# Fourier block MLP on one core: the layer groups in twos, with the 64-row matmuls of two groups side by side

## The reference

```python
xf = jnp.fft.rfft2(x, axes=(1, 2), norm='ortho')          # -> (B, H, 65, 8, 96), complex
o1r = relu(xr @ w1[0] - xi @ w1[1] + b1[0])
o1i = relu(xi @ w1[0] + xr @ w1[1] + b1[1])
o2r = o1r @ w2[0] - o1i @ w2[1] + b2[0]
o2i = o1i @ w2[0] + o1r @ w2[1] + b2[1]
o = softshrink(stack([o2r, o2i]), 0.01)
out = jnp.fft.irfft2(complex(o), s=(H, W), norm='ortho') + x
```

## Time and profile before

| | |
|---|---|
| median of 3 runs | 5096.25 us (5095.34 to 5097.84) |
| span of the profiled execution | 5094.2 us; no time of its own is given beside the span |
| granted TensorE clock, mean | 0.993 |
| TensorE busy | 4981.3 us (98%) |
| VectorE busy | 3816.7 us (75%) |
| ScalarE busy | 2996.3 us (59%) |
| GpSimd busy | 1436.3 us (28%) |
| DMA moved | 430.24 MB, mean 84 GB/s |

### The profile page before, as it was taken

How to read it: one execution, slowest core, us unless ns; L and a number is a source line. 1 busy time by engine, 2 the same in 40 slices (tenths; PEclk the granted TensorE clock), 3 DMA queues, 4 the chain that set the end, 5 groups by cost and what they waited for, 6 DMA issues and landing times.

```text
span 5094.2 us, 113221 instructions
## 1 busy us (share of the span) xinstructions
PE 4981.3 (98%) x40000; PEld 4673.3 (92%) x40000; DVE 3816.7 (75%) x6159; ACT 2996.3 (59%) x5409; POOL 1436.3 (28%) x905
## 2 busy tenths in 40 slices
PE   6999999999999999999999999999999999999997
PEld 6999999999999999999999999999999999999996
DVE  5777777777777777777777777777777777777876
ACT  4555655556655566555566555665556655556653
POOL 3033223332123332233321333312333123332220
PEclk8999999999999999999999999999999999999998
DMA  5044423444323443234442344432344323444233
GB/s 114 12 94 105 98 59 69 91 105 105 68 57 87 105 105 87 56 81 94 105 105 52 70 90 105 106 70 62 79 105 106 86 61 78 92 105 105 61 73 72
DMA packets 1699712, 430.24 MB, mean 84 GB/s; under 512 B 1698848, under 2 KB 1698976, under 8 KB 1699104
## 3 DMA queue, kind: packets, MB, share of 16 engines
q1 hardware_dynamic: 1696768, 421.83, 37.5%
q10 hardware_dynamic: 2336, 0.59, 0.1%
HBM read 220.84 MB, written 201.33 MB: 83 GB/s over the span
## 4 chain that ended last, share of the span: by engine, by line
PE 96%; DVE 2%; issue 1%; SPq 1%; ACT 0%; DMA 0%; DVEq 0%; ACTq 0%
PE psum L807 15%; PE psum L778 14%; PE psum L822 14%; PE psum L760 13%; PE psum L849 13%; PE psum L832 9%; PE psum L790 7%; PE psum L859 3%; PE psum L860 3%; PE psum L861 3%; DVE mixed L655 1%; SPq L387 1%; DVE spectrum L628 0%; PE psum L840 0%; PE psum L839 0%
## 5 line engine op out<-in xcount | busy, mean ns | idle before, releaser
L655 DVE COPY mixed<-psum 128x768 f32<-128x768 f32 (+1 forms) x512 | 477.4, 932 | 700.0 <-PE psum L790 700.0
L541 ACT ACTIVATE sums_high<-psum 128x512 fp32r<-128x512 f32 x768 | 459.2, 599 | 731.3 <-PE psum L849 731.2
L807 PEld LDWEIGHTS psum<-mats,mixed 128*128 128x128 f32 x6272 | 744.0, 191 | 121.2 <-issue 113.1
L807 PE MATMUL psum<-mats,mixed 128*128 128x128 f32 x6272 | 841.8, 283 | 0.0
L778 PE MATMUL psum<-w_whole,whole 128*128 128x192 f32 x4160 | 782.3, 330 | 40.9 <-ACT whole L482 11.4
L822 PE MATMUL psum<-w2t,hidden 128*128 128x192 f32 x4160 | 771.7, 328 | 0.0
L849 PE MATMUL psum<-mats,spectrum 128*128 128x128 f32 x6144 | 743.7, 275 | 3.1 <-DVE spectrum L663 1.6
L760 PE MATMUL psum<-mats,x 128*128 128x128 f32 x6144 | 704.9, 277 | 33.6 <-DVE x L582 17.8
L760 PEld LDWEIGHTS psum<-mats,x 128*128 128x128 f32 x6144 | 696.0, 193 | 40.9 <-issue 23.0
L778 PEld LDWEIGHTS psum<-w_whole,whole 128*128 128x128 f32 x4160 | 673.3, 197 | 60.6 <-issue 33.7
L849 PEld LDWEIGHTS psum<-mats,spectrum 128*128 128x128 f32 x6144 | 714.5, 192 | 4.1 <-DVE sums_low L701 2.0
(11 more groups left out here) (76 smaller groups left out, 7800.7 us busy)
## 6 DMA issues: line engine op xcount, KB each, us to landing
x<-x SPq DMA_DIRECT2D x736, 192.0 KB, 2.9
out<-x SPq DMA_DIRECT2D x736, 192.0 KB, 2.5
x<-x SPq DMA_DIRECT2D x736, 64.0 KB, 2.6
out<-x SPq DMA_DIRECT2D x736, 64.0 KB, 2.2
x<-x SPq DMA_DIRECT2D x32, 144.0 KB, 2.7
out<-x SPq DMA_DIRECT2D x32, 144.0 KB, 2.3
w2t<-L_conv_w SPq DMA_DIRECT2D x124, 36.0 KB, 1.8
x<-x SPq DMA_DIRECT2D x64, 48.0 KB, 2.4
```

The lines of the kernel that those rows point to most:

```text
L655: copied = dve.tensor_copy(mixed[s % 2][:, 0:k], both_b(s)[:, 0:k])
L807: last = pe.matmul(out[tile], flat[:, tile * SIZE:(tile + 1) * SIZE], mat(FH), start=True, stop=True)
```

## The change

The groups are handled in rounds of two, ten rounds (`ROUNDS`) in a unit. Round j takes the even group 2j and the odd groups around it. What it does:

- TensorE has one stretch of 64-row matmuls in a round: `stage_b_halved(2j)`, `stage_d_middle(2j - 2)`, `stage_d_middle(2j - 1)`, `stage_b_halved(2j + 1)`. The steps over 128 rows follow in the order first layer of the odd group, `stage_c` even, outer tiles of the odd group before, first layer of the next even group, `stage_c` odd, outer tiles even.
- For odd groups the halved part now opens the sums in PSUM and the whole part closes them; likewise the outer tiles of odd groups now close the second layer's sums and increment `d_done`. `stage_b_halved` of an odd group above 1 waits for `b_copied` of the even group just before it.
- ScalarE and VectorE follow the new order. `gather` is split in `gather_whole` and `gather_halved`.
- Each `unfold_step` is cut in two (16 steps over 5 or 6 rows), and `spare(k)` places four steps in each round from round 1 on: the 16 unfold steps in rounds 1 to 4, the six prepare steps in rounds 5 and 6.

No matmul is added or taken away. The core of the diff (ScalarE's round first, then the unfold step, VectorE's round, TensorE's stages and TensorE's round):

```diff
+ROUNDS = NS // 2 + 2
+
+
+def even_group(j):
+    return 2 * j if 0 <= 2 * j < NS else None
+
+
+def odd_group(j):
+    return 2 * j + 1 if 0 <= 2 * j + 1 < NS else None
...
+                for j in range(ROUNDS):
+                    if j == 0:
+                        gather_halved(1)
+                        gather_whole(1)
+                    if even_group(j - 1) is not None:
+                        hide(even_group(j - 1))
+                    if odd_group(j - 2) is not None:
+                        exceed(odd_group(j - 2))
+                    if j > 0 and odd_group(j) is not None:
+                        act.wait_ge(b_done, n * NS + 2 * j)
+                        gather_whole(odd_group(j))
+                        gather_halved(odd_group(j))
+                    if odd_group(j - 1) is not None:
+                        hide(odd_group(j - 1))
+                    if j == ROUNDS - 1:
+                        act.wait_ge(flip_done, n + 1)
+                        act.activation(U[:, 0:BLOCK, SIZE + 2:].rearrange("p c k -> p k c"), bank_flip,
+                                       ACT.Copy).then_inc(flip_copied, 1)
+                    if even_group(j - 1) is not None:
+                        exceed(even_group(j - 1))
+                    if even_group(j + 1) is not None:
+                        act.wait_ge(b_done, n * NS + (2 * j + 1))
+                        gather_whole(even_group(j + 1))
+                        gather_halved(even_group(j + 1))
...
-                x_unit, (lo, hi) = xs[par], PIECES[k // 2]
+                p, what = divmod(k, 4)
+                x_unit, (lo, hi) = xs[par], PIECES[p]
+                lo, hi = ((lo, lo + 5), (lo + 6, hi))[what % 2]
...
+                    dve.wait_ge(unfold_even, n * (2 * NP) + (2 * p + what - 1))
...
+                    if what == 3:
+                        done.then_inc(unfolded, 1)
...
+                for j in range(ROUNDS):
+                    if odd_group(j - 1) is not None:
+                        mix(odd_group(j - 1))
+                    if even_group(j - 1) is not None:
+                        hide_middle(even_group(j - 1))
+                    if 0 < j:
+                        spare(4 * j - 4)
+                        spare(4 * j - 3)
+                    if odd_group(j - 2) is not None:
+                        shrink(odd_group(j - 2))
+                    if odd_group(j - 1) is not None:
+                        seed(odd_group(j - 1))
+                        hide_middle(odd_group(j - 1))
+                    if 0 < j:
+                        spare(4 * j - 2)
+                    if even_group(j) is not None:
+                        mix(even_group(j))
+                    if 0 < j:
+                        spare(4 * j - 1)
+                    if even_group(j - 1) is not None:
+                        shrink(even_group(j - 1))
+                    if even_group(j) is not None:
+                        seed(even_group(j))
...
+                opens = s % 2 == 0
...
-                    pe.matmul(bank_b(s, k), whole[s % 2][:, k // 2, :, k % 2], w1_whole[par][:, :, :].rearrange("p r o -> p (r o)"),
-                              start=k % 2 == 0, stop=False, skip_group_check=True)
+                    last = pe.matmul(bank_b(s, k), whole[s % 2][:, k // 2, :, k % 2], w1_whole[par][:, :, :].rearrange("p r o -> p (r o)"),
+                                     start=opens and k % 2 == 0, stop=not opens, skip_group_check=True)
+                if not opens:
+                    last.then_inc(b_done, 1)
...
+                opens = s % 2 == 1
...
+                    if opens and s > 1:
+                        pe.wait_ge(b_copied, n * NS + s)
...
-                                             start=False, stop=True, skip_group_check=True)
-                last.then_inc(b_done, 1)
+                                             start=opens and i == 0, stop=not opens, skip_group_check=True)
+                if not opens:
+                    last.then_inc(b_done, 1)
...
+                ends = s % 2 == 1
                 pe.wait_ge(relu_done, n * (2 * NS) + (2 * s + 1))
-                pe.wait_ge(seeded, n * NS + (s + 1))
+                if not ends:
+                    pe.wait_ge(seeded, n * NS + (s + 1))
...
+                ends = s % 2 == 0
                 pe.wait_ge(middle_done, n * NS + (s + 1))
+                if not ends:
+                    pe.wait_ge(seeded, n * NS + (s + 1))
...
-                for s in range(NS + 2):
-                    if s < NS:
-                        stage_b_whole(par, n, s)
-                    if s == NS:
+                for j in range(ROUNDS):
+                    if odd_group(j - 1) is not None:
+                        stage_b_whole(par, n, odd_group(j - 1))
+                    if j == ROUNDS - 1:
+                        stage_d_outer(par, n, odd_group(j - 2))
+                    if even_group(j - 1) is not None:
+                        stage_c(n, even_group(j - 1))
+                    if j < ROUNDS - 1 and odd_group(j - 2) is not None:
+                        stage_d_outer(par, n, odd_group(j - 2))
+                    if even_group(j) is not None:
+                        stage_b_whole(par, n, even_group(j))
+                    if odd_group(j - 1) is not None:
+                        stage_c(n, odd_group(j - 1))
+                    if j == ROUNDS - 1:
                         flip(n)
-                        stage_c(n, NS - 1)
-                    if s >= 2:
-                        stage_d_outer(par, n, s - 2)
-                        stage_d_middle(par, n, s - 2)
-                    if s < NS:
-                        stage_b_halved(par, n, s)
-                    if 1 <= s < NS:
-                        stage_c(n, s - 1)
+                    if even_group(j - 1) is not None:
+                        stage_d_outer(par, n, even_group(j - 1))
+
+                    if even_group(j) is not None:
+                        stage_b_halved(par, n, even_group(j))
+                    if even_group(j - 1) is not None:
+                        stage_d_middle(par, n, even_group(j - 1))
+                    if odd_group(j - 1) is not None:
+                        stage_d_middle(par, n, odd_group(j - 1))
+                    if odd_group(j) is not None:
+                        stage_b_halved(par, n, odd_group(j))
```

More of the change, by code:

```diff
@@ L469, in _, with gather_whole @@
         def _(act):
-            def gather(s):
-                w, h, first = whole[s % 2], halved[s % 2], GROUPS[s][0]
+            def gather_whole(s):
+                w, first = whole[s % 2], GROUPS[s][0]
+                j = 2 + 2 * first
                 if s == REAL:
@@ L509, in layers @@
                 act.wait_ge(dve_copied, (n + 1) * len(A_DVE))
[L510 removed]
+                gather_whole(0)
                 act.wait_ge(w_loaded[par], (m + 1) * W_LOADS * 16)
[L512 to L534 removed]
@@ L535, in layers, with hide @@
-                act.wait_ge(flip_done, n + 1)
-                act.activation(U[:, 0:BLOCK, SIZE + 2:].rearrange("p c k -> p k c"), bank_flip,
-                               ACT.Copy).then_inc(flip_copied, 1)
+                def hide(t):
+                    tiles = hidden[t % 2]
+                    act.wait_ge(c_done, n * NS + (t + 1))
+                    act.activation(tiles[:, 0, 0:pairs(t)], bank_c[:, 0, 0:pairs(t)], ACT.Relu,
+                                   bias=b1t[par][:, 0:1]).then_inc(relu_done, 1)
+                    k = pairs(t) if None not in GROUPS[t] else 1
+                    act.activation(tiles[:, 1, 0:k], bank_c[:, 1, 0:k], ACT.Relu,
+                                   bias=b1t[par][:, 2:3]).then_inc(relu_done, 1)
@@ new lines, in exceed @@
+                def exceed(t):
+                    act.wait_ge(d_done, n * NS + (t + 1))
+                    if t >= 1:
+                        act.wait_ge(shrunk, n * NS + t)
+                    act.activation(excess[:, :, 0:rows_d(t)], parts_d(t), ACT.Relu,
+                                   bias=over[:, 0:1]).then_inc(excess_done, 1)
+                for j in range(ROUNDS):
[22 more added lines that the diff above has]
+                        gather_halved(even_group(j + 1))
@@ new lines, in mix @@
+                def mix(s):
+                    k = pairs(s)
+                    dve.wait_ge(b_done, n * NS + (s + 1))
+                    if s == 1:
+                        for i in range(2):
+                            flat = mixed[s % 2][:, i].rearrange("p y (r o) -> p y r o", r=2)
+                            copied = dve.tensor_copy(flat, both_b(s, i))
+                    else:
+                        copied = dve.tensor_copy(mixed[s % 2][:, 0:k], both_b(s)[:, 0:k])
+                    copied.then_inc(b_copied, 1)
@@ new lines, in hide_middle, with shrink @@
+                def hide_middle(t):
+                    dve.wait_ge(c_done, n * NS + (t + 1))
```

(26 more changed lines are left out.)

107 lines of the change are left out of this document (27 added, 80 removed).

## The result

The changed kernel takes **5007.70 us** (median of 4 runs, 5006.03 to 5008.48), the kernel before 5097.04 (4 runs, 5095.34 to 5097.84), so it is 89.3 us faster. The ratio is 0.9823, with a 95% interval of 0.9812 to 0.9835. The profiled execution has a span of 5004.2 us at a granted clock of 0.994, so 90.0 us less than the span before.

A forecast was written before the change was run, and what follows sets the result against it. TensorE, busy 98%, was taken to bound the kernel. Per unit -3.60 - 0.73 + 1.44 = -2.89 us, -92.5 over 32 units, -91.5 with the tail, gave 5005 us, range 4980 to 5038.

The forecast's parts named there:

- nine stretches less: TensorE: ten 64-row stretches a unit in place of 19, each entry and exit costing 0.40 us; 3.60 us a unit saved.
- wait before the outer tiles of group 0 removed: TensorE, start of a unit: the idle time before group 0's outer tiles goes, 0.20 us a unit saved.
- wait at the first layer of group 4 removed: TensorE's wait for group 3's copy goes, as `stage_d_outer(1)` now stands between; 0.53 us a unit saved.
- (a): Rounds 3 to 7: odd group's `stage_b_halved` waits for the even group's copy, 0.09 us each, 0.45 us a unit added.
- (b): Round 2: the same wait with only six pairs of matmuls between; 0.44 us a unit added.
- (c): `stage_c(1)`, behind group 2's short first layer, waits for both `hidden` operations of group 0; 0.55 us a unit added.
- rival (1): Nothing saved at joined edges, the 0.40 us belonging to every change of stage; only waits remain, 5120 us; chance 0.04.
- M + 1.55 and M + 1.46: When matmuls after the copy flow, with and without wait, in us from M, start of `stage_b_halved(2j)`'s last matmul.
- Free 0.6 us early: VectorE in a round: 4.16 us of work against TensorE's 4.79, so free 0.6 us before the even group's copy.
- Rival (2): VectorE late for the wait inside the stretch, half unfold steps costing nearly what whole ones do; 5235 us; chance 0.04.
- (3): Rival: all waits are covered, the releases after VectorE's copy and ScalarE's work being quicker; 4959 us; chance 0.06.
- (4): Rival: new waits twice as long, plus 0.2 us of delay at the start of the inverse; 5057 us; chance 0.12.

The follow-up runs named there:

- experiment 1: Changed kernel with the even group's halved first layer moved ahead of the outer tiles, giving 18 stretches a unit instead of 10: 5076.67 us.
- Experiment 9: Changed kernel with the copy of even groups 4 to 14 shared, VectorE copying one bank of the sums and ScalarE the other: 4977.46 us.
- experiment 5: Changed kernel with an unused VectorE addition of 256 columns ahead of the even group's copy in rounds 2 to 8: 5030.90 us.
- experiment 6: Changed kernel with an unused VectorE addition of 768 columns ahead of the even group's copy in rounds 2 to 8: 5063.50 us.
- experiment 2: Changed kernel with eight whole unfold steps, two in a round, in place of 16 half steps: 5004.91 us.
- experiment 10: Changed kernel with the even copies shared by VectorE and ScalarE, group 0's outer tiles ahead of `stage_c(1)`, and whole unfold steps: 4967.16 us.

## Why the prediction was right

Predicted were 5005 us in a range of 4980 to 5038; measured are 5007.70. By its own steps, in us a unit:

| step | predicted | measured |
|---|---|---|
| nine stretches less | -3.60 | -3.41 |
| wait before the outer tiles of group 0 removed | -0.20 | -0.18 |
| wait at the first layer of group 4 removed | -0.53 | -0.53 |
| (a) copy inside the stretch, rounds 3 to 7 | +0.45 | +0.58 |
| (b) round 2 | +0.44 | +0.44 |
| (c) `stage_c(1)` | +0.55 | +0.55 |
| first layer behind `stage_c` | none | -0.12 |
| sum | -2.89 | -2.67 |
| `layers`, measured as a whole | | -2.71 |

*The edges.* The mechanism was right: experiment 1 gives the cost back together with the idle loads. The size was a little off: in and out cost 0.398 us before and 0.415 after (from the starts of the single matmuls, beyond the rate), and 19 x 0.398 - 10 x 0.415 = 3.41. The difference stands in the step from the first matmul to the second, where a load is exposed: 0.105 and 0.102 us on the way in and out before, 0.111 and 0.111 after. After, first-layer matmuls stand at nearly every end of a stretch, and their loads last 0.19 to 0.20 us, against 0.18 to 0.19 for the others; that this is why was not tested. The rule weighed in the prediction, by which a load overlaps only across row groups, does not hold in this trace: with the loads of same rows exposed in every order, joining stretches would have left the kernel at 5120 us. That also was rival (1).

*The waits added.* (b) and (c) came out as worked out from the trace before. Term (a) was sized too small: 0.116 us a round in place of 0.09, which is 0.13 us a unit and 4 us in all. The two ends of the difference, M + 1.55 and M + 1.46 in the prediction, are 1.56 and 1.46 by the single matmuls of the rounds 3 and 1, so each was within about 0.01; a term that is the small difference of two long chains takes their whole error. What (a) costs is the 0.11 us of one exposed load, not a stall of the matmuls. Experiment 9 shows that these waits are the copy's length.

*VectorE.* "Free 0.6 us early" is 0.67 us in the trace, and the experiments 5 and 6 show by delays of 0.45 and 0.95 us that this is cover and not chance. Half a step is 0.95 us where I had 0.97. Rival (2) needed a half step of more than 1.35 us and was far off. That the cut steps cost nothing is right, but that they are needed was not said and is not so (experiment 2).

*What the sum left out.* In the kernel before, the second matmul of `stage_b_whole` comes 0.009 us late wherever that stage follows `stage_c`, fourteen times a unit; in the new order it follows `stage_c` once. That is 0.12 us a unit which the prediction did not have. With it the terms add up to 2.67 of the 2.71 us; 0.04 are not placed. The 1 us for the cut steps behind the last unit was not needed: from the end of the last `layers` to the end of the span it is 73.97 us before and 73.99 after.

*How near, and why.* The errors at the edges (0.19), in (a) (0.13) and at the outer tiles (0.02) are 0.34 us a unit, some 11 us too fast. Against them stand the 0.12, the 0.04 not placed, and the 0.10 between the median unit (2.71) and the span (90.0 / 32 = 2.81), some 8 us, and the 1 us behind the last unit. The span came out 1.5 us above the predicted one, and the median stands 3.5 us above the profiled span where 2.05 was assumed. That all this leaves less than 3 us is luck; the errors in either direction alone would have stayed inside the range.

*The rivals.* Nothing of (1) is seen. (3), all waits covered, would have been 4959 us; the three waits are there, and experiment 10 comes within 8 us of it by taking most of them away. (4), twice as long, is contradicted at (b) and (c), and at the start of the inverse nothing is added: from the first middle matmul of group 16 to the first matmul of `stage_a` it is 0.84 us before and after.

## What to carry to other kernels

A busy share of 98% can hide 2 to 3% that an order can win (130 of 5097 us here): lay one step out by instruction rates, and look at what is left where the loads stand idle. Where the cost is in a change of kind (here 64 against 128 rows), count the changes and let the order share them, then price each wait that the joined stretch creates, since in it the producer and the consumer of a copy move close together; splitting that copy over two engines that had room brought a third as much again. Cover measured as idle time is good for work that uses the engine alone, so look at what else runs at that moment before you place a delay or a step there.

## What was unexpected of the hardware

VectorE's additions with both inputs in SBUF take longer here when GpSimd is at work. The addition over 256 columns of experiment 5 takes 0.42 us (mean of 147, 0.41 to 0.43) where GpSimd is idle and 1.34 us (mean of 77, up to 2.04) where GpSimd runs; that over 768 columns of experiment 6 takes 0.95 against 1.68 us, up to 2.59. The same holds in the kernel after itself for the sign steps of the weights (L653), which have one input: 0.20 us beside an idle GpSimd (50 of them), 0.94 on average and up to 1.60 beside a busy one (78). Its timeline:

```profile
1970.67 0.21 DVE L653 TENSOR_SCALAR w2t<-w2t 32x96 f32<-32x96 f32 x1
...
1977.02 1.54 POOL L456 TENSOR_TENSOR x<-x,doubled 128x640 f32<-128x640 f32 x1
1977.59 2.58 DVE L653 TENSOR_SCALAR w2t<-w2t 32x96 f32<-32x96 f32 x2
1978.64 1.47 POOL L450 TENSOR_TENSOR doubled<-x 128x768 f32<-128x768 f32 x1
```

The first step takes 0.21 us alone, two more take 2.58 beside GpSimd. The Trainium skill, "GPSIMD Engine Reference", section 1 ("Specifications"), says that GpSimd shares its SBUF interfaces with VectorE, with contention for VectorE instructions with two SBUF inputs or in a 2-port mode; for the additions the rows agree, and the page gives no size. Which mode the sign steps run in no row shows. The copies, which read PSUM, were not seen longer: the one of experiment 5 at 1983.50, in the middle of GpSimd's additions, takes 0.96 us as in a quiet round, and in the kernel after the 191 copies of 768 columns beside a busy GpSimd take 0.96 us like the other 289. The unfold steps, which have two SBUF inputs, never meet a busy GpSimd in the kernel after (none of 512), so this change did not touch on it. An order that moves them into the rounds of GpSimd's work might; no run here tried it.
